# A third buffer, in SBUF, for the exponentials that a state-space scan reads

## The reference

```
x = x + layernorm(mamba(layernorm(x)))
x = x + layernorm(ffn(layernorm(x)))

mamba:  hidden, gate = split(x @ W_in + b_in)              # 512 -> 2 x 1024
        c = silu(causal_conv4(hidden, conv_w) + conv_b)
        dt_in, B, C = split(c @ W_x, [128, 144])           # 128 + 16 + 16
        delta = softplus(dt_in @ W_dt + b_dt)              # 1024 channels
        for n in 16 states:  dA = exp(delta * A[:, n])     # A = -exp(a_log)
              h_t = dA_t * h_(t-1) + (delta*c)_t * B_t,n   # scan over time
              y  += h * C[:, n]
        out = ((y + c * d_param) * silu(gate)) @ W_out + b_out
ffn:    two Walsh-Hadamard transforms around silu(x @ W_gate.T) * (x @ W_up.T), then @ W_down.T
```

## Time and profile before

| | |
|---|---|
| median of 3 runs | 2645.28 us (2644.28 to 2645.57) |
| the profiled execution: its time, its span | 2648.76 us, 2647.0 us |
| busy PE, DVE, POOL, ACT | 97%, 85%, 77%, 69% of the span |
| from the first scan to the last | 70.7 to 2467.9 us |
| one chunk | 150.2 us (16 silu of the gate, from 235.6 to 2488.0) |

### The profile page before, as it was taken

The page is one execution under the profiler, slowest core; times in us unless marked ns, Lnnn a source line. Parts: engine busy times, 40 slices in busy tenths (PEclk is TensorE's granted clock), DMA queues, the critical chain, the costliest instruction groups (busy, mean ns, idle before and its releaser), DMA issues.

```text
span 2647.0 us, 46296 instructions
## 1 busy us (share of the span) xinstructions
PE 2574.1 (97%) x16048; PEld 2187.0 (83%) x16048; DVE 2243.8 (85%) x2573; ACT 1815.0 (69%) x3935; POOL 2046.4 (77%) x1691
## 2 busy tenths in 40 slices
PE   7999989999999999999999999999999999989998
PEld 5566668989888888989888898989888898978888
DVE  6898998899898898899899889989889889889522
ACT  4776777677777777777777767777777777755322
POOL 6776879788787979888797979888797988877222
PEclk9999999999999999999999999999999999989999
DMA  5654256657666666666666665766666666646675
GB/s 181 214 204 167 100 166 219 224 196 241 210 236 215 216 221 209 238 204 232 220 224 221 215 225 199 240 212 227 225 216 221 207 221 214 224 176 230 239 288 190
DMA packets 165209, 564.41 MB, mean 213 GB/s; under 512 B 17264, under 2 KB 19696, under 8 KB 132976
## 3 DMA queue, kind: packets, MB, share of 16 engines
q1 hardware_dynamic: 164976, 561.44, 61.5%
HBM read 527.30 MB, written 34.08 MB: 212 GB/s over the span
## 4 chain that ended last, share of the span: by engine, by line
PE 78%; DVE 10%; ACT 7%; issue 3%; DMA 1%; POOL 0%; SPq 0%; DVEq 0%; ACTq 0%; POOLq 0%
PE pF L726 21%; PE hT L633 14%; PE pM L651 13%; PE pD L742 10%; PE pM L703 8%; DVE h L1180 5%; DVE acc L1193 3%; PE pM L673 3%; PE pD L766 3%; ACT decay L986 2%; PE decay L726 2%; PE hT L625 1%; PE pF L766 1%; ACT delta L963 1%; ACT delta L958 1%
## 5 line engine op out<-in xcount | busy, mean ns | idle before, releaser
L1180 DVE TENSOR_TENSOR_SCAN h<-decay,dbx 128x512 f32<-128x512 f32 x1024 | 1200.1, 1206 | 73.7 <-ACT decay L986 41.5
L1362 POOL TENSOR_TENSOR dbx<-u,bb 128x2048 f32<-128x2048 f32 (+1 forms) x272 | 1179.6, 4338 | 37.5 <-DVE h L1180 35.5
L986 ACT ACTIVATE decay<-delta,a_neg 128x255 f32<-128x255 f32 x2048 | 874.0, 468 | 301.8 <-DVE h L1180 295.0
L1193 DVE SCALAR_TENSOR_TENSOR acc<-hT,bcT,acc 128x1024 f32<-128x1024 f32 x480 | 610.3, 1271 | 141.1 <-PE hT L633 137.5
L726 PE MATMUL pF<-fxT_hi,wug 128*128 128x256 f32 x3712 | 725.3, 288 | 0.7 <-issue 0.7
L726 PEld LDWEIGHTS pF<-fxT_hi,wug 128*128 128x128 f32 x3712 | 595.9, 192 | 1.3 <-issue 1.1
L633 PEld LDWEIGHTS hT<-ident,h 128*128 128x128 f32 x4096 | 472.8, 141 | 140.8 <-issue 89.5
L633 PE MATMUL hT<-ident,h 128*128 128x128 f32 x4096 | 535.4, 274 | 33.3 <-DVE acc L1193 22.1
L726 PE MATMUL pF<-fxT_lo,wug 128*128 128x256 f32 x1856 | 525.7, 283 | 0.0
L651 PE MATMUL pM<-xnT,w_in 128*128 128x256 f32 x2016 | 479.9, 381 | 4.1 <-ACT hid L906 2.6
L651 PEld LDWEIGHTS pM<-xnT,w_in 128*128 128x128 f32 x2016 | 367.3, 191 | 51.6 <-issue 5.0
(11 more groups left out here) (177 smaller groups left out, 2674.9 us busy)
## 6 DMA issues: line engine op xcount, KB each, us to landing
wug<-scratch_ug SPq DMA_DIRECT2D x243, 1024.0 KB, 4.8
wd<-scratch_wd SPq DMA_DIRECT2D x243, 512.0 KB, 4.1
w_in<-in_W_in SPq DMA_DIRECT2D x252, 256.0 KB, 2.9
bb<-scratch_bc SPq DMA_DIRECT2D x128, 256.0 KB, 4.7
xb<-in_hidden_states SPq DMA_DIRECT2D x16, 512.0 KB, 5.2
xr<-in_hidden_states SPq DMA_DIRECT2D x16, 512.0 KB, 5.8
out<-xr SPq DMA_DIRECT2D x15, 512.0 KB, 3.7
kept_ug<-scratch_ug SPq DMA_DIRECT2D x7, 1024.0 KB, 8.0
```

Source lines behind the costliest of these rows:

```text
L986: e = act.activation(da[q % 2][:, i, 1:], delta[c % 2][:, dt, 1:], ACT.Exp, scale=a_neg[:, dt, n:n + 1])
L1180: dve.tensor_tensor_scan(row(h[n % 2][:, tiles, :]), row(da[q % 2][:, :, :]), row(dbx[n % 2][:, tiles, :]), 0.0, ALU.mult, ALU.add).then_i ...
L1193: dve.scalar_tensor_tensor(acc[c % 2][:, tb, :], hT[:, :], cn, acc[c % 2][:, tb, :], ALU.mult, ALU.add).then_inc(acc_done, 1)
L1362: pool.tensor_tensor(dbx[n % 2][:, tiles, :], u[:, tiles, :], rows, ALU.mult).then_inc(done if restarts(c) else prod_done, 1)
```

## The change

`da` gets a third buffer, `decay2`, in SBUF instead of PSUM. The quarters take the three buffers in turn: quarter `q` of state `n` of chunk `c` takes number `(64 c + 4 n + q) mod 3`. ACT waits for the scan three quarters before, where it waited for the one two before. To make room in SBUF, `dt_rows` and `dtin` become parts of `tap[0]`. No instruction changes its place in the order of any engine. The memset of column 0 is made for the third buffer too.

```
-        dt_rows = sb("dt_rows", [P, TB, DTR])
-        dtin = sb("dtin", [P, T])
+        dt_rows = tap[0][:, 0, :].rearrange("p (a k) -> p a k", a=TB)
+        dtin = tap[0][:, 1, :]
...
-        da = [pb(f"decay{i}", [P, DQ, T]) for i in range(2)]
+        da = [pb(f"decay{i}", [P, DQ, T]) for i in range(2)] + [sb("decay2", [P, DQ, T])]
+
+        def da_of(c, n, q):
+            return da[(NQ * (NST * c + n) + q) % len(da)]
+
...
-                    if c == 0 and n == 0 and q < 2:
-                        act.wait_ge(da_zeroed, 2)
+                    if c == 0 and n == 0 and q < len(da):
+                        act.wait_ge(da_zeroed, len(da))
                     else:
-                        act.wait_ge(scan_done, NQ * (NST * c + n) + q - 1)
+                        act.wait_ge(scan_done, NQ * (NST * c + n) + q - len(da) + 1)
                     for i in range(DQ):
                         dt = DQ * q + i
-                        e = act.activation(da[q % 2][:, i, 1:], delta[c % 2][:, dt, 1:], ACT.Exp, scale=a_neg[:, dt, n:n + 1])
+                        e = act.activation(da_of(c, n, q)[:, i, 1:], delta[c % 2][:, dt, 1:], ACT.Exp, scale=a_neg[:, dt, n:n + 1])
                     e.then_inc(da_done, 1)
...
-                dve.tensor_tensor_scan(row(h[n % 2][:, tiles, :]), row(da[q % 2][:, :, :]), row(dbx[n % 2][:, tiles, :]), 0.0,
+                dve.tensor_tensor_scan(row(h[n % 2][:, tiles, :]), row(da_of(c, n, q)[:, :, :]), row(dbx[n % 2][:, tiles, :]), 0.0,
                                        ALU.mult, ALU.add).then_inc(scan_done, 1)
```

## The result

The changed kernel takes 2963.22 us (median of 5 runs, 2962.72 to 2964.25), the kernel before 2645.28 us: a ratio of 1.1201, 95% interval 1.1188 to 1.1214, 318 us slower. The forecast was 2860 us, with a range of 2730 to 2990.

The account below looks back on a forecast made before the run. PE was taken as the bound, with DVE close behind. Holds of 400 us less 188 taken up by DVE's idle time gave +212 us on the profiled 2648.8, said as 2860 us, 80% range 2730 to 2990.

Parts of the forecast that it names:

- The mechanism: In the scan stretch, each DVE scan with two SBUF inputs waits for what is left of POOL's SBUF-reading instruction.
- Rival 1: DVE's scans take no turns with POOL; only the gain is left, 2636 to 2649 us; chance 9%.
- Rival 2: DVE gets in ahead and POOL's slack takes up most of the turns: +60 to +120 us, 2710 to 2770; chance 12%.
- The small parts: ACT's writes to SBUF, at most 20 us and hidden; one small memset; the shared place in tap[0], costing nothing.
- The removal: Up to 41.5 us of DVE's waits on exponentials go; PE's idle time lets this give 13 us at most.
- The holds: Waits of DVE's decay2 scans for POOL's instructions: 5.05 us in three states, 431 us in all, taken as 400.
- The absorption: DVE's 250 us of idle time in the scan stretch takes up 188 us of the waits, bounds half to all.
- rival 3: POOL also becomes the bound through held time in the tap stretch: about 2980 us, up to 3070; chance 10%.
- PE's clock: A sign of being wrong: PE's clock, granted in full before, falls because PE pauses, adding an uncounted amount.
- the forecast's own mechanism: DVE's scans are held and late adds stop PE: 2760 to 2955 us, chance 69%.

Follow-up runs that it names:

- the four quarters: Four kernels giving the SBUF buffer to only one quarter (0, 1, 2 or 3) of each state, the rest using two PSUM buffers: 3035.9, 2940.4, 2745.7, 2754.7 us.
- the memsets: POOL's product replaced by a POOL memset of the same tile: 2669.0 us with the changed kernel's three buffers, 2643.6 us with two in PSUM.
- the three memset kernels: Two PSUM buffers plus DVE memsets of 400 columns, one before every scan, three before every third, or four before each state's first: 2807.4, 2928.9, 2946.1 us.
- quarter 1: Changed kernel, but decay2 in SBUF serves only the second scan of each state, the others taking two PSUM buffers in turn: 2940.4 us, ratio 1.1113.
- quarter 0: Changed kernel, but decay2 in SBUF serves only the first scan of each state, the others taking two PSUM buffers in turn: 3035.9 us, ratio 1.1467.
- quarter 3: Changed kernel, but decay2 in SBUF serves only the last scan of each state, the others taking two PSUM buffers in turn: 2754.7 us, ratio 1.0410.
- quarter 2: Changed kernel, but decay2 in SBUF serves only the third scan of each state, the others taking two PSUM buffers in turn: 2745.7 us, ratio 1.0382.

## Why the prediction was right, and what was mis-sized

1. **The mechanism.** DVE's scans with two SBUF inputs and POOL's reading instructions take turns by whole instructions. Forecast from butterflies at the start of the trace alone; shown by the timeline at 439 us, by the four quarters, and by the memsets. Rival 1 (a scan takes no turns) is out: 2536 ns against 1203. Rival 2 (POOL pays for most) is out as well: its product has a mean of 4637 ns, 40 more than before, though its busy time as a whole is up by 200 us.
2. **The small parts.** The shared place costs nothing, shown (1.0002). ACT's writes to SBUF: the mean of all went from 468 to 478 ns, a third of them thus to 498, as the tap row said; ACT waited for scans 418 us beside it, so it was hidden.
3. **The removal.** I gave it up to 13 us; measured with a third PSUM buffer it is nothing, and the waits it was to shorten are the same 45.7 us. With `decay2` they were 32.4 us in a kernel where ACT had more time.
4. **The holds.** Forecast 2.81, 1.64, 0.3 and 0.3 us for quarters 0 to 3, 5.05 us in three states. The trace after has (means of the scans that read `decay2`, less 1.206) 2.23, 1.49, 0.92 and 0.68 us, 5.3 us in three states. I had 431 us from this and lowered it to 400 for POOL's smaller share; it was 452. The step mis-sized is that quarters 2 and 3 fall behind the product. Of their 79 and 58 us of holds, 65 and 34 are under the product itself, which POOL had begun late, and 8 and 15 under `gating`; the tap adds, which I had named, have 1 us in all.
5. **The absorption,** the term most off. I let DVE's idle time take up 188 us of 250, and it took up 118. The bounds of half to all, 125 to 250, were just missed. DVE's extra work by itself is taken up as I said, 182 to 192 us, shown by the three memset kernels. What stands beside the loss is POOL: where its tap adds are not held (quarter 1, 731 ns) 172 us are taken up, nearly as with memsets; where they are held (902 ns with quarter 0, 815 in the changed kernel) it is 40 and 116. The chain then runs through POOL (25% and 16%), and ACT, which works in order, waits 100.5 us for tap adds before it can go on to exponentials, against 42.9 before (148.5 with quarter 0). The rows of before and of quarter 3:

```profile
ACT conv L929 <- POOL conv L1419: 42.9, 35, 2.7
```

```profile
ACT conv L942 <- POOL conv L1433: 129.5, 55, 4.1
```

   With quarter 3 the tap adds are short (752 ns), and yet ACT waits 129.5 us for them, POOL has 23% of the chain, and 90 us are taken up. With the memset for POOL's product they are long (808 ns), and ACT waits 5.8 us. So the length of the tap adds is not what counts, but how late POOL gets to them. This was the mechanism of rival 3, to which I gave a separate case above 2980 us; it is in the result with some 70 us (188 - 118) at the most. It is read from kernels side by side and was not isolated: quarter 2 takes up only 113 us with 4% of POOL in the chain, which this does not explain, though quarters 2 and 3 also added less than half as much work, 214 and 199 us.
6. **PE's clock.** The mean granted clock was 0.996 before and 0.974 after. The one thing I named as adding more than I had counted did happen. The clock has two levels here, 1.2 and 2.4 GHz, so these means stand for 21 us at the lower one before and (1 - 0.974) x 2 x 2962 = 154 us after. At half the speed PE can lose at most half of what was added, some 67 us (an estimate, and a bound). Three chunks of the changed kernel whose quarters fall on the buffers alike, with the silu of the gate at either end:

```profile
762.65:934.11 171.46, 158.93 (x985) 137.34 (x983) 161.59 (x157) 110.57 (x243) 137.24 (x102) 0.96 0.57 191
1278.78:1442.30 163.52, 154.15 (x988) 133.05 (x986) 156.35 (x157) 110.56 (x242) 137.43 (x93) 0.99 0.59 200
1790.34:1957.69 167.35, 157.15 (x986) 135.66 (x985) 156.93 (x157) 110.87 (x243) 140.78 (x114) 0.97 0.58 195
```

   and DVE's scans alone in them:

```profile
762.65:934.11 171.46, 101.77 (x64) 0.96 0.57 191
1278.78:1442.30 163.52, 96.50 (x64) 0.99 0.59 200
1790.34:1957.69 167.35, 96.96 (x64) 0.97 0.58 195
```

   Over the whole span PE is busy 90% of the time, where it was 97%, with 203 us of waits for adds, up to 4.1 us each, where it had 22. The chunk with the clock at 0.96 is 8 us longer than the one at 0.99, but its scans were held 5.3 us longer too, so this pair does not isolate the clock. The third chunk, with scans nearly as short as the second's and the clock at 0.97, is 3.8 us longer than the second. In the kernel with quarter 0 in SBUF the same comparison shows no effect:

```profile
1141.36:1315.36 174.00, 155.44 (x989) 133.02 (x988) 158.32 (x158) 109.13 (x244) 140.31 (x114) 0.99 0.55 188
1315.36:1488.93 173.57, 157.66 (x972) 135.60 (x971) 157.48 (x156) 108.99 (x242) 136.36 (x93) 0.96 0.56 195
1838.27:2011.39 173.12, 154.56 (x981) 132.08 (x980) 157.83 (x157) 109.09 (x243) 140.39 (x115) 0.99 0.56 191
2011.39:2184.99 173.60, 157.69 (x972) 135.35 (x971) 157.70 (x156) 109.01 (x243) 136.52 (x93) 0.96 0.58 195
```

   Its scans are busy 98.2 to 98.9 us in each of these chunks, and the chunks at 0.96 are as long as those at 0.99. They differ in POOL's small instructions as well (93 against 114), so this is a strong hint and no proof that the clock does not explain the kernel in which least was taken up. With memsets the clock was 0.99 at nearly the length of the changed kernel. How the 70 us of point 5 divide between POOL's lateness and the clock stays open.

The forecast of +212 us is 106 short of the measured 318: 452 in place of 400 for the holds, and 118 in place of 188 for what was taken up, make 122 of it; the rest is that other groups of DVE overlap more, its busy time being up by 434 rather than 452. The measured 2963 us lie above the 2955 us that bound the forecast's own mechanism. The wider range, up to 2990, holds them because it left room for part of rival 3, and that much of the hit is luck: it covered two terms that were both mis-sized in the same direction.

## What to carry to other kernels

Before a DVE operand is moved from PSUM to SBUF, count the SBUF tensors that the instruction then reads. In this kernel a scan with two of them took turns with POOL's instructions that read SBUF, and the price was what was left of POOL's instruction when it came, so the product of 4.6 us that was released by the last scan was the worst neighbour. It can be read in advance from the two timelines laid side by side. A wait of an engine that runs ahead (ACT's 295 us) is no reason for another buffer; put the buffer where it costs nothing once, and see whether the time moves.

## What the runs showed of the hardware

- A TENSOR_TENSOR_SCAN of 128x512 takes 1.2 us whether `decay` is in PSUM or, when POOL is not reading, in SBUF. Under POOL's reads it reached 5.7 us (up to 4.6 us of product and its own time); 99 that were not held had a median of 1.21 us.
- A POOL memset of 128x2048 takes 1.81 us, a product of that size 4.60 us, and only the latter holds such a scan.
- The turns hold POOL as well: 8 columns took 0.94 us in place of 0.21, and the tap adds' longest 1.75 us against a median of 0.73.
